# Second slice's token rows modulated as rows on GpSimd; its router weights modulated instead of its turned rows

## The reference

```
mod = silu(c) @ wmod                     # c: 16 x 128, six rows of 128 for each batch
sa, ca, ga, sb, cb, gb = six rows; ga, gb pushed away from zero (|.| >= 0.25)
h = layernorm(x) * (1 + ca) + sa
x = x + ga * attn(h)                     # gated delta rule: 16 heads of 8, a state of 8x8 each,
                                         # one step per token, then rms norm and Wo
h = layernorm(x) * (1 + cb) + sb         # second modulation: cb scales, sb shifts, by batch
logits = h @ router_w + router_b         # 8 experts
route = softmax(logits); e = argmax      # top-1 expert of each token
y = (silu(a) * g) @ w2[e] * max(route)   # a, g = halves of h @ w1[e], 128 -> 2*512
x = x + gb * y
```

## Time and profile before

| What | Value |
|---|---|
| median of three runs | 484.82 us (483.6 to 489.69) |
| the profiled execution | 484.07 us, its span 482.1 us |
| TensorE matmul busy | 374.5 us, 78% of the span, 2505 instructions |
| VectorE busy | 383.1 us, 79%, 1166 |
| ScalarE busy | 277.2 us, 58%, 624 |
| GpSimd busy | 265.5 us, 55%, 329 |
| mean granted TensorE clock | 0.897 |
| chain that ended last | PE 38%, DVE 27%, issue 10%, POOL 10%, ACT 6%, DMA 4% |

### The profile page before, as it was taken

The page is one execution under the profiler, slowest core; times in us unless marked ns, Lnnn a source line. Parts: engine busy times, 40 slices in busy tenths (PEclk is TensorE's granted clock), DMA queues, the critical chain, the costliest instruction groups (busy, mean ns, idle before and its releaser), DMA issues.

```text
span 482.1 us, 8634 instructions
## 1 busy us (share of the span) xinstructions
PE 374.5 (78%) x2505; PEld 323.3 (67%) x2505; DVE 383.1 (79%) x1166; ACT 277.2 (58%) x624; POOL 265.5 (55%) x329
## 2 busy tenths in 40 slices
PE   2967683936889997875968948889997878999970
PEld 1323321735777777875968948889897867999970
DVE  5868999999999999999979999677755324459734
ACT  3698858936366465767467372845554536665620
POOL 1027236999999668949491786132224555333340
PEclk9988977969979997995985978999999998999995
DMA  8186899990000008704000011252121122415106
GB/s 229 40 104 115 100 125 139 107 98 1 0 1 1 2 0 302 223 7 84 0 1 1 1 34 40 55 106 62 35 93 61 45 83 66 120 44 139 33 28 179
DMA packets 48861, 35.00 MB, mean 73 GB/s; under 512 B 10992, under 2 KB 45072, under 8 KB 48688
## 3 DMA queue, kind: packets, MB, share of 16 engines
q1 hardware_dynamic: 45424, 28.28, 30.6%
q0 software_dynamic: 3392, 6.18, 4.3%
HBM read 15.26 MB, written 10.27 MB: 53 GB/s over the span
## 4 chain that ended last, share of the span: by engine, by line
PE 38%; DVE 27%; issue 10%; POOL 10%; ACT 6%; DMA 4%; SPq 2%; another core or an unknown queue 1%; ACTq 0%; POOLq 0%; DVEq 0%
PE bank L854 13%; PE bank L604 6%; PE bank L871 6%; DVE U L1698 5%; DVE S L1711 5%; DVE p L1692 4%; DVE p L1705 4%; PE bank L661 4%; POOL big L967 2%; POOL prod_o L298 2%; PE bank L751 2%; PE bank L665 1%; ACT ph L1116 1%; PE bank L606 1%; POOL placed_y L1070 1%
## 5 line engine op out<-in xcount | busy, mean ns | idle before, releaser
L661 PE MATMUL bank<-prod_o,ID 128*128 128x128 f32 x512 | 75.5, 309 | 30.6 <-POOL prod_o L305 18.7
L854 PE MATMUL bank<-Q,p 128*128 128x128 f32 x736 | 95.9, 277 | 2.9 <-issue 2.0
L854 PEld LDWEIGHTS bank<-Q,p 128*128 128x128 f32 x736 | 90.3, 193 | 4.0 <-issue 2.5
L661 PEld LDWEIGHTS bank<-prod_o,ID 128*128 128x128 f32 x512 | 70.6, 220 | 33.4 <-POOL prod_o L305 22.0
L1070 POOL DMA_INDIRECT placed_y<-Q,place x46 | 44.2, 960 | 80.4 <-ACT Q L1424 31.2
L1228 ACT ACTIVATE p<-S,GAM 128x64 f32<-128x64 f32 x126 | 48.3, 410 | 66.7 <-DVE S L1711 66.0
L298 POOL TENSOR_TENSOR prod_o<-Q,ST 128x1024 f32<-128x1024 f32 x28 | 60.0, 2143 | 30.3 <-PE bank L665 30.0
L1417 ACT ACTIVATE p<-big 128x1024 f32 x46 | 48.5, 1057 | 43.2 <-PE bank L854 40.4
L1711 DVE TENSOR_REDUCE S<-p 128x64 f32<-128x320 f32 x126 | 56.2, 480 | 0.0
L1698 DVE TENSOR_REDUCE U<-p 128x32 f32<-128x288 f32 x128 | 52.4, 444 | 0.0
L1692 DVE TENSOR_TENSOR p<-S,bank 128x256 f32<-128x256 f32 x128 | 49.1, 414 | 0.7 <-ACT bank L1223 0.7
(11 more groups left out here) (253 smaller groups left out, 749.7 us busy)
## 6 DMA issues: line engine op xcount, KB each, us to landing
big<-in_L_ffn_w_dram SPq DMA_DIRECT2D x1, 4096.0 KB, 14.1
big<-big SPq DMA_DIRECT2D x16, 192.0 KB, 4.8
Q<-sorted_h SPq DMA_DIRECT2D x46, 64.5 KB
sorted_h<-ZERO SPq DMA_DIRECT2D x2, 1472.0 KB, 18.2
X<-in_L_attn_x_dram SPq DMA_DIRECT2D x8, 256.0 KB, 4.7
big<-big SPq DMA_DIRECT2D x16, 128.0 KB, 5.3
K<-placed_y SPq DMA_DIRECT2D x8, 256.0 KB
out_dram<-X SPq DMA_DIRECT2D x8, 256.0 KB, 2.4
```

The costliest lines, as they stand in the source:

```text
L661: pe.matmul(ps, ID[:, :], prod_o[:, k % 2, i, :], start=(i == 0), stop=False, skip_group_check=True)
L854: m = pe.matmul(bank[(1, 6)[g % 2] + k][:, c * P:(c + 1) * P], W1E[g % 2][:, f:f + P], XST[:, g % 3, :], start=True, stop=True)
```

## The change

- The scale (1 + cb) and shift sb are made a second time, as 16 x 128 rows (two products on TensorE, copied by ScalarE to MROW), stored by SP to mod_h in DRAM, and spread from there to all partitions: SHIFTS and SCALES, four DMAs of 128 partitions x 4 KB.
- GpSimd modulates the rows of slice 1 itself: XNB times SCALES plus SHIFTS into H2, two instructions of 128 x 512 a quarter, between its row stores of tiles 4 to 7 (MOD_AT = 4).
- GpSimd makes router weights for each batch (RWS[1] = weights times scale, RWS[0] = weights times shift). The logits of slice 1 are normalised rows times RWS[1], added in PSUM to a product of ones with RWS[0].
- The turned rows are only copied (copy_turned, ScalarE), shift2, turn_back and rows are gone for slice 1, and both turns come earlier (tiles 7 and 8), routing at tile 10 instead of 12, the scatter after row store 8 instead of 10.
- VectorE normalises all sixteen tiles at tile 7.
- The outputs of half 1 are scaled and moved by GpSimd, those of half 0 by VectorE (ahead of gate_u(0)) and SP alone.
- The two-bank scheme for turned tiles and results begins at tiles 15 and 13 instead of 17 and 15.

```diff
-    F_ATTEND, F_ROOT, F_TURN = (3, 4), 6, (8, 10)
-    SHARE = HB // 2
-    F_ROUTE = F_TURN[1] + 2
+    F_ATTEND, F_ROOT, F_TURN = (3, 4), 6, 7
+    F_ROUTE = F_TURN + 3
+    MOD_AT = F_ROOT - 2
-    YACT = F_ROUTE + 1
+    YACT = F_ROUTE + 3
...
+        SHIFTS = [K_[1][:, 0:P, :]..., K_[0][:, P:2 * P, :]...]
+        SCALES = [PD[h]... for h in range(NHALF)]
+        RWS = [WP[:, j, :].rearrange("p (b e) -> p b e", b=B) for j in range(2)]
...
+            sp.wait_ge(sem("mod_ready"), 7)
+            for j in range(2):
+                sp.dma_start(mod_h[j]..., MROW[:, j, :]).then_inc(sem("mod_rows"), 16)
...
             move_outputs(sp, 0, [0])
+            def spread_rows(half, j, rows):
+                sp.dma_start(rows..., mod_h[j]...[half * HB * D:(half + 1) * HB * D].broadcast_to([P, HB * D]))
+            sp.wait_ge(sem("mod_rows"), 32)
+            sp.wait_ge(sem("ov_ready1_", 0), 1)
+            spread_rows(0, 0, SHIFTS[0])
+            for h in range(NHALF):
+                sp.wait_ge(sem("prod_ready", h), PG)
+                sp.wait_ge(sem("weights_in"), NHALF)
+                spread_rows(h, 1, SCALES[h])
...
                 if g == MOVE - 1:
-                    move_outputs(sp, 1, [0], range(SHARE))
-                if g == MOVE:
-                    move_outputs(sp, 1, [1])
+                    move_outputs(sp, 1, [0])
+                    spread_rows(1, 0, SHIFTS[1])
...  (TensorE)
             def weigh_experts(k):
-                shifted(pe, k)
+                if s == 0:
+                    shifted(pe, k)
+                else:
+                    pe.wait_ge(sem("turn_copied"), q + 1)
+                    pe.wait_ge(sem("xst_ready"), F_TURN + 4 + q // 2)
+                if k == 4:
+                    pe.wait_ge(sem("router_ready"), 2)
+                    pe.matmul(LG_BANK[s], ONES[:, :], RWS[0]..., start=True, stop=False)
...
+                        m = pe.matmul(lg_t, H2T[:, k % 2, i * P:(i + 1) * P], RWS[1][:, t, :], start=False, stop=True)
...
-                if g in F_TURN:
-                    for q in (0, 1):
-                        turn_rows2(4 + 2 * F_TURN.index(g) + q)
-                if g - 1 in F_TURN:
-                    for q in (0, 1):
-                        weigh_experts(4 + 2 * F_TURN.index(g - 1) + q)
-                        turn_back(4 + 2 * F_TURN.index(g - 1) + q)
+                if g == F_TURN:
+                    for q in (0, 1):
+                        turn_rows2(4 + q)
+                if g == F_TURN + 1:
+                    for q in (0, 1):
+                        weigh_experts(4 + q)
+                        turn_rows2(6 + q)
+                if g == F_TURN + 2:
+                    for q in (2, 3):
+                        weigh_experts(4 + q)
...  (GpSimd)
+            def modulate_rows(k):
+                s, q = divmod(k, 4)
+                h, first = q // 2, q % 2 * 4
+                rows = H2[s][h][:, first:first + 4, 0:D]
+                pool.wait_ge(sem("xn2_ready", s), 4 * (q + 1))
+                if k == 4:
+                    pool.wait_ge(sem("mod_rows"), 32 + 16 * 4)
+                link(pool.tensor_tensor(rows, XNB[:, 4 * q:4 * q + 4, :], SCALES[h][:, first:first + 4, :], ALU.mult))
+                pool.tensor_tensor(rows, rows, SHIFTS[h][:, first:first + 4, :], ALU.add).then_inc(sem("h2_evac"), 1)
...
-            move_outputs(pool, 1, [0], range(SHARE, HB), "ot_pool")
+            modulate_router()
+            pool.wait_ge(sem("roots_ready"), 2 * NHALF + NTIME + 3)
+            scale_outputs(pool, 1, 1)
+            move_outputs(pool, 1, [1])
             for g in range(NTIME * NF):
...
+                if MOD_AT <= g < MOD_AT + 4:
+                    modulate_rows(g - MOD_AT + 4)
...  (ScalarE, ahead of silu(g))
-                if g - 2 in F_TURN:
+                if g - 1 in (F_TURN, F_TURN + 1):
                     for q in (0, 1):
-                        rows(4 + 2 * F_TURN.index(g - 2) + q)
+                        copy_turned(4 + 2 * (g - 1 - F_TURN) + q)
...  (VectorE)
                 if g == 0:
                     now(rsqrt(sm[:, 2, :], O_EPS, sm[:, 4, :], sm[:, 4, :], sm[:, 5, :]))
+                    scale_outputs(dve, 1, 0)
...
-                    scale(1, second_tile, XNB, "xn2_ready", range(NT // 2))
-                if g == F_ROOT + 2:
-                    scale(1, second_tile, XNB, "xn2_ready", range(NT // 2, NT))
-                if g - 1 in F_TURN:
-                    for q in (0, 1):
-                        shift2(4 + 2 * F_TURN.index(g - 1) + q)
+                    scale(1, second_tile, XNB, "xn2_ready", range(NT))
...
-                if g < NHALF:
-                    scale_outputs(dve, 1, g)
```

More of the change, by code:

```diff
@@ L249, in adaln_block @@
         GB = WOG
+        SHIFTS = [K_[1][:, 0:P, :].rearrange("p t d -> p (t d)").rearrange("p (n d) -> p n d", n=HB),
+                  K_[0][:, P:2 * P, :].rearrange("p t d -> p (t d)").rearrange("p (n d) -> p n d", n=HB)]
+        SCALES = [PD[h][:, :, :].rearrange("p c t -> p (c t)").rearrange("p (n d) -> p n d", n=HB) for h in range(NHALF)]
+        RWS = [WP[:, j, :].rearrange("p (b e) -> p b e", b=B) for j in range(2)]
         H2T = K_[0][:, 0:P, :].rearrange("p t d -> p (t d)").rearrange("p (r t) -> p r t", r=2)
@@ L259, in scale_outputs, with move_outputs @@
                 .then_inc(sem(f"ov_ready{h}_", s), 1)
-        def move_outputs(queue, s, halves, blocks=range(HB), landed_in="ot_in"):
+        def move_outputs(queue, s, halves):
             for h in halves:
@@ L268, in move_outputs @@
                     queue.wait_ge(sem("att_ps", 0), 4)
-                for b in blocks:
-                    queue.dma_start(OT[h][:, b, :], OV[s][h][b * H:(b + 1) * H, :, :]).then_inc(sem(f"{landed_in}{h}_", s), 16)
+                for b in range(HB):
+                    queue.dma_start(OT[h][:, b, :], OV[s][h][b * H:(b + 1) * H, :, :]).then_inc(sem(f"ot_in{h}_", s), 16)
         def bank_states(g, h):
@@ L536, in _ @@
             move_outputs(sp, 0, [0])
+            def spread_rows(half, j, rows):
+                sp.dma_start(rows.rearrange("p n d -> p (n d)"),
+                             mod_h[j].rearrange("(a x) -> a x", a=1)[:, half * HB * D:(half + 1) * HB * D].broadcast_to([P, HB * D]))\
+                    .then_inc(sem("mod_rows"), 16)
+            sp.wait_ge(sem("mod_rows"), 32)
[5 more added lines that the diff above has]
+                spread_rows(h, 1, SCALES[h])
             for g in range(NTIME * NF):
@@ L579, in _ @@
             m.then_inc(sem("mod_ps"), 1)
+            for i, j in enumerate((3, 4)):
+                m = pe.matmul(bank[6][0:B, i * D:(i + 1) * D], CT_[:, :], WM[:, j, :], start=True, stop=True)
+            m.then_inc(sem("mod_ps"), 1)
             def turn_rows(k):
@@ L711, in attend @@
                 if q % 2 == 0:
[L712 to L714 removed]
+                    pe.wait_ge(sem(f"ot_in{h}_", s), 16 * HB)
                 if s == 1 and q == 0:
@@ L993, in decay_queries, with modulate_router @@
                 pool.wait_ge(sem("q_decayed", h), s + 1)
+            def modulate_router():
+                pool.wait_ge(sem("wo_in"), 16 * 4)
+                pool.wait_ge(sem("proj_evac"), 4 * NB)
+                for j in range(2):
+                    pool.tensor_tensor(RWS[j], RW[:, :].unsqueeze(1).broadcast_to([P, B, E]),
+                                       MOD[:, 2 + j, :].unsqueeze(2).broadcast_to([P, B, E]), ALU.mult).then_inc(sem("router_ready"), 1)
+            def modulate_rows(k):
[7 more added lines that the diff above has]
+                pool.tensor_tensor(rows, rows, SHIFTS[h][:, first:first + 4, :], ALU.add).then_inc(sem("h2_evac"), 1)
             def place_rows(s):
@@ L1090, in _, with copy_mod_rows @@
             act.activation(MOD[:, :, :], m4, ACT.Copy).then_inc(sem("mod_ready"), 1)
-            act.wait_ge(sem("mod_ready"), 2)
+            act.wait_ge(sem("mod_ready"), 3)
             for j in (1, 3):
                 act.activation(MOD[:, j, :], MOD[:, j, :], ACT.Identity, bias=1.0).then_inc(sem("mod_ready"), 1)
+            def copy_mod_rows():
+                act.wait_ge(sem("mod_ps"), 4)
+                for j in range(2):
+                    act.activation(MROW[:, j, :], bank[6][0:B, j * D:(j + 1) * D], ACT.Identity, bias=float(j)).then_inc(sem("mod_ready"), 1)
             asked = [0]
@@ L1166, in _ @@
             root(yy[:, :], mv[:, :, 1], LN_EPS)
+            copy_mod_rows()
             shift(0)
```

49 lines of the change are left out of this document (32 added, 17 removed).

## The result

The changed kernel took 495.63 us (median of four runs, 490.33 to 495.94), the kernel before 485.97 beside it (four runs, 483.6 to 489.69). The ratio on record is 1.0142, 95% interval 1.0089 to 1.0195 (the two medians alone give 1.020). So it is slower, by less than the 2% that the prediction takes as its bound, and outside the range of 478 to 489. The profiled execution took 495.66 us; its span is 493.9, 11.8 more than before.

A forecast was written before the change was run, and what follows sets the result against it. TensorE was taken to bound the chain from 320 to 401 us, with 12.2 us lost around the scatters. Terms -0.8 + 0 - 0.3 = -1.1 us on 484.07 gave 483.0, its own range 481.5 to 484.5, outer range 478 to 489.

The forecast's parts named there:

- Turning back: TensorE's chain: sixteen transposes of slice 1 go (2.2 us), one product for the shift's logits comes (0.24); net -2.0 us.
- Attention: Slice 1's attention: half 0 lands at 321.3, a new wait of 1.1 us; half 1's wait of 0.98 goes; +0.1.
- The two scalings: Scalings of output halves 0 (VectorE) and 1 (GpSimd): a shared port lock may make them run one after the other.
- The first rival: GpSimd takes the port first at the scalings, everything behind 2.8 us later: +1.7 in all, 485.8 us; chance 0.22.
- Norm and turn: Turn of quarters 0 and 1 at tile 7: 2.4 us of new TensorE waits, 1.12 us gone; +1.3 us.
- "so nothing" for the modulation: GpSimd's eight row products for slice 1, 10.2 to 11.4 us, were to add nothing to the time.
- the fourth rival: The change buys nothing: tile 7's waits take the 2.0 us, slowed normalisations up to +2.4; 484 to 485.5; chance 0.10.
- The cover that I named: Modulation done at about 353, scatter's places at 359.9: 6 us of slack before the scatter would be delayed.
- Scatter stretch: Tiles 13 to 23, beside GpSimd's scatters and waiting stores: about 40 us; -0.3 us, bounds -5 and +4.
- rival 3: Lossy stretch grows by more waiting stores or the spreads: +4, 487 us; tile 13 to 23 in 44 us; chance 0.15.
- rival 2: Lossy stretch gives time back: -5 more, 478 us; tile 13 to 23 in 35 us; chance 0.18.
- Spreads: Four 512 KB transfers of scale and shift rows, 2.5 us each: bounds 0 and +2.5, taken as 0.

The follow-up runs named there:

- the mended kernel: Changed kernel with outputs scaled and moved as before, last spread at tile 13, modulation in one block behind all sixteen normalisations: 1.0059 of the kernel before.
- the outputs' part alone: Kernel before, with VectorE scaling half 0 and SP moving all of it, GpSimd scaling and moving half 1, no spread rows: 1.0090 of the kernel before.
- The old way of the outputs: Changed kernel with VectorE scaling both halves, SP and GpSimd sharing half 0's moves, SP moving half 1: 1.0139 of the kernel before.

## Why the prediction was wrong

**Turning back, -2.0: borne out together with the turn.** The second piece of the mended kernel is 0.6 us shorter (0.5 to 0.6 in all four profiles of mended kernels); -2.0 and the +1.3 of the turn make -0.7.

**Attention, "+0.1": the step that failed first.** It measured +3.7 and +4.4. The step said that half 0 would be there at 321.3, from a last move begun at 318.7 and a landing 2.6 us behind it. That landing was of a move behind which GpSimd had no moves under way. Here the eighth move was begun at 319.45, since one issue took 1.69 us, and it landed 3.70 us later (4.57 in the outputs' part alone), beside GpSimd's eight; I had treated the two queues as free of each other. The wait became 3.10 instead of 1.1, and the lower clock behind it added 1.1 us on attention and 0.6 on the next eight products. With the wait of 0.98 that goes, these add up to 3.8, close to the measured 3.7. The old way of the outputs removes it. That the landing is late because of GpSimd's moves is inferred: it took 3.1 to 4.6 us in the five profiles with GpSimd's eight under way, and half 1's last move, with none of them, 2.4 to 2.5 in the thirteen with the old way, but no run took GpSimd's moves away and left all else.

**The two scalings: right.** VectorE began at 311.84, GpSimd at 311.88, and GpSimd's took 4.66 instead of 2.86: it stood for about VectorE's 2.04 and then ran. The first rival, which needed GpSimd first, did not occur. By the rule of the Trainium skill, "SBUF — State Buffer", section "SBUF: two separate sides" (an exclusive lock for a whole instruction), that is what had to come.

**Norm and turn, "+1.3", and "so nothing" for the modulation: the other step that failed.** I had set the lock only against the two scalings. The modulation costed at nothing has its products beside VectorE's normalisations and routing, and the fourth rival named this at "up to +2.4". It was four products and not two: 4.6 us. As the rows read, each delay keeps the normalisations there long enough to meet the next product. TensorE got 4.0 us of idle at the turn, of which 2.1 are left in the mended kernel: the first wait has its predicted size (1.69 for 1.8), the second is 2.32 instead of 0.6. Then come the lower clock (0.83 from 340 to 350) and 1.0 us more at the rank. The piece is 4.3 us longer instead of 0.7 shorter. The cover that I named, 6 us before the scatter, was real and beside the point: the first scatter came at 368.29, 2.1 us later than before and not 6 earlier, because routing itself was late. What hid GpSimd's 10 us was time of GpSimd, not of the port.

**The rule on the steps that were held.** The routing steps are tensor-tensor instructions with both inputs in SBUF, as the rule has it. The normalisations have one tensor in SBUF and a scale and shift for each partition, and they were held too (0.34 us in the median, 2.08 the longest). The same section of the Trainium skill's page has a second case for the lock, a VectorE instruction in a two-port mode, and counts tensor_scalar among those that can enter one. That they were held fits this case; in which mode they ran, no run shows. The prediction had taken only the first case from the page.

**Scatter stretch, "-0.3": neither shown nor refuted.** The two profiles of the changed kernel give +4.1 and 0.0. From tile 13's first matmul to tile 23's they have 45.0 and 40.7 us: the first is at rival 3's 44, the second at the forecast's 40, and rival 2's 35 does not show. The bound of +4 was passed by 0.1 in one profile. In the four profiles of mended kernels the piece is 46.3 to 47.3, 1.5 to 2.5 above the one profile of the kernel before and inside the scatter of this piece.

**Spreads, 0:** the ones before 305 us cost nothing (the loop begins at 306.7 to 306.9 as before); the last costs 0.5 to 1.2 us by single profiles.

So the terms with no other engine beside them held as far as they can be read (-0.7 for turning and norm, 0.68 at the rank), and the sum failed in the two where a second queue or the port was shared. The chance of 0.10 for the fourth rival, with its limit of +2.4, was the worst of the numbers, and the low clock behind a new wait stood in no term at all.

## What to carry to other kernels

Before work on GpSimd is costed at nothing, list VectorE's SBUF instructions that run in the same stretch: each product of GpSimd here added about its length to those that it met, and if they sit on the chain, place the products in a block where VectorE idles or reads PSUM (the gate products, one input in PSUM, kept their 0.68 us beside GpSimd's products in the mended kernel). A landing time read from a row holds for as many transfers under way as that row had. A new wait of some 3 us on TensorE is to be priced with the slower instructions behind it: here 1.7 to 1.9 us more.

## What the runs showed of the hardware

- A VectorE tensor-scalar of 128x128 from SBUF to SBUF (0.34 us, two scalars for each partition) took up to 2.08 us beside GpSimd's tensor-tensor products, and a tensor-tensor of the same size with both inputs in SBUF 1.87 instead of 0.29.
- TensorE's granted clock was 0.65 over 4 us after 2.89 us of idle, 0.83 over 10 us around 1.69 + 2.32 us of idle. In the mended kernel, with 1.70 + 0.37 us of idle, it was 1.00 from 338 to 348, and the instructions behind it keep their usual length.
- With sixteen indirect DMAs from GpSimd, 1.27 us apart in their bursts, eleven tiles take 44.8 us instead of 32.9. In some stretches TensorE's matmuls come singly, 0.7 us apart; in others, with indirect DMAs as close, it has no gap (383.9 to 390.0 in the kernel with plain DMAs). With plain DMAs of the same size in the scatters' place the stretch takes 37.1. Through what the indirect form reaches TensorE no run shows.
